# An adaLN block with linear attention and a mixture of experts on one core: scatters that wait for the one two tiles back, later last logits, full sixth down passes, a reordered first shared slot

## The reference, cut to what matters

```python
x: (4, 1024, 512) f32                       # B, N, C
mod = (silu(c) @ wmod) -> sa, ca, ga, sb, cb, gb     # ga, gb clamped away from 0
h = layernorm(x) * (1 + ca) + sa
x = x + ga * attention(h)                   # 16 heads of 32, relu(q), relu(k), linear:
                                            # (v_pad k^T) q, divided by its last row, then w_proj
h = layernorm(x) * (1 + cb) + sb
scores = sigmoid(h @ gate_w.T)              # 8 experts
idx = top_k(scores + router_bias, 2);  w = scores[idx] / sum(scores[idx])
out = sum_k w_k * (silu(h W1[e]) * (h W3[e])) W2[e]          # inner width 352
shared = (silu(h sw1.T) * (h sw3.T)) sw2.T                   # inner width 704
x = x + gb * (out + shared)
```

## Time and profile before

| | us |
|---|---|
| median of 3 runs | 1271.02 |
| lowest and highest | 1267.22, 1271.38 |
| profiled execution, its own time | 1265.33 |
| its span, first to last instruction | 1263.6 |
| TensorE busy in the span | 1202.6 (95%) |
| VectorE, ScalarE, GpSimd busy | 796.3, 416.6, 480.4 |

### The profile page before, as it was taken

How to read it: one execution, slowest core, us unless ns; L and a number is a source line. 1 busy time by engine, 2 the same in 40 slices (tenths; PEclk the granted TensorE clock), 3 DMA queues, 4 the chain that set the end, 5 groups by cost and what they waited for, 6 DMA issues and landing times.

```text
span 1263.6 us, 25262 instructions
## 1 busy us (share of the span) xinstructions
PE 1202.6 (95%) x9054; PEld 774.5 (61%) x9054; DVE 796.3 (63%) x1575; ACT 416.6 (33%) x873; POOL 480.4 (38%) x408
## 2 busy tenths in 40 slices
PE   7999999999998999999999999999999999999992
PEld 2646666666665666676776767566666555555551
DVE  6557778778765777476675643466666555555552
ACT  4324445444443333333332332222222222222220
POOL 2214566566554454311111102344443444344432
PEclk9999999999999999999999999999999999999996
DMA  7915698898788887453353443766766667777673
GB/s 232 234 44 150 169 220 207 214 231 202 190 209 188 221 201 177 105 131 94 93 141 84 103 128 77 164 126 126 126 126 126 125 126 121 131 126 122 118 108 46
DMA packets 253110, 185.01 MB, mean 146 GB/s; under 512 B 186480, under 2 KB 198768, under 8 KB 252988
## 3 DMA queue, kind: packets, MB, share of 16 engines
q1 hardware_dynamic: 217224, 114.14, 39.1%
q0 software_dynamic: 20512, 45.62, 20.9%
q10 hardware_dynamic: 15256, 23.62, 6.4%
HBM read 87.07 MB, written 52.49 MB: 110 GB/s over the span
## 4 chain that ended last, share of the span: by engine, by line
PE 37%; DMA 28%; issue 13%; POOL 11%; DVE 7%; ACT 2%; SPq 1%; POOLq 0%; ACTq 0%; DVEq 0%
DMA out<-y,slot_row 25%; PE ps_vs L86 3%; PE ps_vs L88 3%; PE ps_vs L87 3%; PE ps_vh L86 2%; PE ps_vh L88 2%; PE ps_vh L87 2%; POOL h L339 2%; PE ps_kh L86 2%; PE ps_kh L87 2%; PE ps_kh L88 2%; POOL xg L347 2%; POOL ol L352 2%; PE ps_qh L88 2%; PE ps_qh L86 2%
## 5 line engine op out<-in xcount | busy, mean ns | idle before, releaser
L428 POOL DMA_INDIRECT out<-y,slot_row x71 | 113.6, 1600 | 248.7 <-DMA out<-y,slot_row 223.1
L86 PE MATMUL ps_o<-w_all,xt 128*128 x568 | 177.8, 313 | 12.6 <-issue 12.3
L87 PE MATMUL ps_o<-w_all,xt 128*128 x568 | 177.6, 313 | 0.0
L88 PE MATMUL ps_o<-w_all,xt 128*128 x568 | 177.5, 313 | 0.0
L854 DVE SCALAR_TENSOR_TENSOR gate_row<-gate_rows,batch_weight,gate_row 128x512 f32<-128x512 f32 x213 | 158.9, 746 | 2.5
L366 POOL DMA_INDIRECT out<-s_sum,row_no x32 | 53.7, 1678 | 220.0 <-DVE s_sum L606 214.6
L861 DVE TENSOR_TENSOR y<-ps_vs,gate_row 128x512 f32<-128x512 f32 x71 | 49.1, 692 | 136.4 <-DMA out<-y,slot_row 118.0
L1105 ACT ACTIVATE at<-ps_y 128x384 f16<-128x384 f32 x71 | 34.9, 491 | 199.2 <-PE ps_y L1323 199.2
L328 POOL TENSOR_TENSOR h<-cen,rows_f 128x512 f32<-128x512 f32 x32 | 40.6, 1267 | 129.8 <-ACT cen L880 112.6
L1111 ACT ACTIVATE gate_row<-gate_rows,batch_weight 128x512 f32<-128x512 f32 x71 | 51.2, 722 | 115.2 <-DVE y L861 103.1
L86 PE MATMUL ps_qh<-ht,wqkv 128*128 128x128 f16 x512 | 87.4, 219 | 1.4 <-DVE wqkv L574 1.4
(11 more groups left out here) (247 smaller groups left out, 3321.3 us busy)
## 6 DMA issues: line engine op xcount, KB each, us to landing
w_stage<-in_w_d ACTq DMA_DIRECT2D x64, 176.0 KB, 2.6
xb<-in_x SPq DMA_DIRECT2D x32, 256.0 KB, 3.2
xr<-in_x SPq DMA_DIRECT2D x32, 256.0 KB, 3.7
out<-x SPq DMA_DIRECT2D x32, 256.0 KB, 3.4
h_d<-hl SPq DMA_DIRECT2D x32, 256.0 KB, 2.5
h2t_d<-h2t SPq DMA_DIRECT2D x32, 256.0 KB, 3.4
s_ht<-h2t_d SPq DMA_DIRECT2D x32, 256.0 KB, 3.5
sstage<-in_sh_flat SPq DMA_DIRECT2D x32, 136.0 KB, 3.2
```

What stands on the lines that cost most here:

```text
L86: nc.tensor.matmul(out, lh, rh, start=first, stop=False, skip_group_check=True)
L87: nc.tensor.matmul(out, lh, rl, start=False, stop=False, skip_group_check=True)
L88: return nc.tensor.matmul(out, ll, rh, start=False, stop=last, skip_group_check=True)
L428: pool.indirect_dma_start(m.out, bass.IndirectOffsetOnAxis(ap=m.slot_row[:, t:t + 1], axis=0), m.y[:, t % Y_RING, :], None, compute_op=ALU ...
```

## The change

Five edits.

1. Scatters. `scatter` of a tile waits for the scatter two tiles back. It waits for the last one too where the expert changes from tile t - 1 to tile t, and for the first tiles. There are two semaphores in turn. The number to wait for comes from a table `wait_for`, which `name_tiles` works out from the expert numbers and GpSimd reads into a register; a step of the semaphore `clear_of_last` follows. Padding slots of even and odd tiles name two different sets of 128 spare rows, so `out` has 128 rows more, and SyncE fills both sets.
2. TensorE's register load of the expert number is made once a tile, ahead of `e_turn`, and kept for `e_down`.
3. The last tile's logits move from the end of slot 43 to behind `up(TAIL_STEPS + 1)`. ScalarE's `logits_out` and the sigmoid, and VectorE's routing parts follow later: sum of logits at step TAIL_STEPS + 2, bias and first pick at + 4, second pick at + 5, weights at + 6, ranks at + 8 (RANK_STEP), run sums at + 14, masks from + 17; the listing ends 6 steps later.
4. The second sixth down pass takes all 128 rows, which adds low activations times low weights.
5. First shared slot (s = 32): GpSimd's `wp_scale` comes behind `o_low`, and ScalarE's `wp_high` moves to the slot's end.

```diff
-TURNS_FROM = TAIL_STEPS + 11
+RANK_STEP = TAIL_STEPS + 8
+TURNS_FROM = RANK_STEP + 9
...
     def scatter(t):
+        if 1 <= t < 3:
+            pool.wait_ge(m.scattered[(t - 1) % 2], 16)
+        if t >= 3:
+            pool.wait_ge(m.scattered[(t - 1) % 2], pool.value_load(m.wait_for[0:1, t:t + 1], min_val=16, max_val=ring_use(t - 1, 2)))
+            pool.sem_inc(m.clear_of_last, 1)
+            pool.wait_ge(m.clear_of_last, t - 2)
+        if t >= 2:
+            pool.wait_ge(m.scattered[t % 2], ring_use(t - 2, 2))
         pool.wait_ge(m.ey_ready, t + 1)
-        at_least(pool, m.scattered, 16 * t)
...
-                                compute_op=ALU.add).then_inc(m.scattered, 16)
+                                compute_op=ALU.add).then_inc(m.scattered[t % 2], 16)
...
+        step(v.tensor_tensor(m.other[:, :], m.eidf[:, 1:SLOT_TILES], m.eidf[:, 0:SLOT_TILES - 1], ALU.not_equal))
+        step(v.scalar_tensor_tensor(out=m.other[:, :], in0=m.other[:, :], scalar=16.0, in1=m.landed_two_back[:, 1:SLOT_TILES],
+                                    op0=ALU.mult, op1=ALU.add))
+        step(v.tensor_copy(m.wait_for[:, 1:SLOT_TILES], m.other[:, :]))
...
-    beside = {TAIL_STEPS: (bias_scores,), TAIL_STEPS + 2: (pick_first,), TAIL_STEPS + 3: (pick_second,), TAIL_STEPS + 4: (weigh,),
-              TAIL_STEPS + 8: (add_runs,), TAIL_STEPS + 9: (place,), TAIL_STEPS + 10: (name_slots,), LIST_STEP: (list_tokens,),
-              LIST_STEP - 1: (name_tiles,)}
-    sum_logits()
+    beside = {TAIL_STEPS + 2: (sum_logits,), TAIL_STEPS + 4: (bias_scores, pick_first), TAIL_STEPS + 5: (pick_second,),
+              TAIL_STEPS + 6: (weigh,), RANK_STEP + 6: (add_runs,), RANK_STEP + 7: (place,), RANK_STEP + 8: (name_slots,),
+              LIST_STEP: (list_tokens,), LIST_STEP - 1: (name_tiles,)}
...
     def e_out(t):
-        at_least(v, m.scattered, 16 * (t - Y_RING + 1))
+        if t >= Y_RING:
+            v.wait_ge(m.scattered[(t - Y_RING) % 2], ring_use(t - Y_RING, 2))
...
-        for b, k in wp_turn(s):
-            wp_high(b, k)
+        if s < TILES:
+            for b, k in wp_turn(s):
+                wp_high(b, k)
...
             convert_weights(q + 1)
-    logits_out(TILES - 1)
+            for b, k in wp_turn(s):
+                wp_high(b, k)
...
     for q in range(TAIL_STEPS, EARLY_STEPS):
         activate(q)
         high(q - 1)
+        if q == TAIL_STEPS + 2:
+            logits_out(TILES - 1)
+        if q == TAIL_STEPS + 3:
+            score()
...
-            nc.tensor.matmul(out, m.s_at[0:SH_HALF, j, 0, tok], m.sh[0:SH_HALF, 1, lo:lo + C], start=False, stop=True, ...)
+            nc.tensor.matmul(out, m.s_at[:, j, 0, tok], m.sh[:, 1, lo:lo + C], start=False, stop=True, ...)
...
         up(q)
-        if q == TAIL_STEPS + 6:
+        if q == TAIL_STEPS + 1:
+            logits(TILES - 1)
+        if q == RANK_STEP:
...
-    e_up(0)
+    expert = expert_of(0)
+    e_up(0, expert)
     down(CHUNKS - 1)
     for t in range(1, SLOT_TILES):
+        following = expert_of(t)
         e_turn(t - 1)
-        e_up(t)
+        e_up(t, following)
-        e_down(t - 1)
+        e_down(t - 1, expert)
+        expert = following
```

More of the change, by code:

```diff
@@ L224, in shared_step @@
             sp.wait_ge(m.s_gb_loaded, 48)
-            sp.dma_start(m.out[T:T + P, :], m.s_gb[:, 0, :]).then_inc(m.spare_stored, 16)
+            for j in range(2):
+                sp.dma_start(m.out[T + j * P:T + (j + 1) * P, :], m.s_gb[:, 0, :]).then_inc(m.spare_stored, 16)
         if j == 4 and n in (BT // 2 + 1, BT + 1):
@@ L448, in gpsimd_program @@
         gather(t + G_RING + 1)
-    pool.wait_ge(m.scattered, 16 * SLOT_TILES)
+    for j in range(2):
+        pool.wait_ge(m.scattered[j], ring_uses(SLOT_TILES, j, 2))
 def vector_program(nc, m, v):
@@ L808, in list_tokens @@
         step(v.tensor_scalar(m.weightf[:, :], m.weightf[:, :], 0.0, None, ALU.is_le))
-        step(v.tensor_scalar(m.rowf[:, :], m.tokenf[:, :], -1.0, m.spare_row[:, 0:1], ALU.mult, ALU.add))
+        step(v.scalar_tensor_tensor(out=m.rowf[:, :], in0=m.tokenf[:, :], scalar=-1.0, in1=m.spare_row[:, 0:SLOT_TILES], op0=ALU.mult, op1=ALU.add))
         step(v.tensor_tensor(m.rowf[:, :], m.rowf[:, :], m.weightf[:, :], ALU.mult))
@@ L1076, in scalar_program, with score @@
             convert_weights(q + 1)
-    logits_out(TILES - 1)
-    for j in range(X2_RING):
-        act.wait_ge(m.x2_stored[j], ring_uses(TILES, j, X2_RING))
-    for j in range(2):
-        act.wait_ge(m.hl2_stored[j], ring_uses(TILES, j, 2))
-    for j in range(H2T_RING):
-        act.wait_ge(m.h2t_stored[j], ring_uses(TILES, j, H2T_RING))
-    act.wait_ge(m.logits_ready, 1)
-    act.activation(m.scores[:, :, :], m.logits[:, :, 0:E], ACT.Sigmoid).then_inc(m.scores_ready, 1)
+            for b, k in wp_turn(s):
+                wp_high(b, k)
+    def score():
+        for j in range(X2_RING):
+            act.wait_ge(m.x2_stored[j], ring_uses(TILES, j, X2_RING))
+        for j in range(2):
+            act.wait_ge(m.hl2_stored[j], ring_uses(TILES, j, 2))
+        for j in range(H2T_RING):
+            act.wait_ge(m.h2t_stored[j], ring_uses(TILES, j, H2T_RING))
+        act.wait_ge(m.logits_ready, 1)
+        act.activation(m.scores[:, :, :], m.logits[:, :, 0:E], ACT.Sigmoid).then_inc(m.scores_ready, 1)
     for q in range(TAIL_STEPS, EARLY_STEPS):
@@ L1244, in down @@
             nc.tensor.matmul(out, m.s_at[:, j, 0, tok], m.sh[:, 0, lo:lo + C], start=False, stop=False, skip_group_check=True)
-            nc.tensor.matmul(out, m.s_at[0:SH_HALF, j, 0, tok], m.sh[0:SH_HALF, 1, lo:lo + C], start=False, stop=True, skip_group_check=True).then_inc(m.sy_done, 1)
+            nc.tensor.matmul(out, m.s_at[:, j, 0, tok], m.sh[:, 1, lo:lo + C], start=False, stop=True, skip_group_check=True).then_inc(m.sy_done, 1)
     pe.wait_ge(m.rep_done, KC)
@@ L1284, in tensor_program @@
             project_out(t - 1)
-        logits(t - 3)
+        if t - 3 < TILES - 1:
+            logits(t - 3)
     for q in range(TAIL_STEPS, EARLY_STEPS):
         up(q)
-        if q == TAIL_STEPS + 6:
+        if q == TAIL_STEPS + 1:
+            logits(TILES - 1)
+        if q == RANK_STEP:
             pe.wait_ge(m.both_ready, 1)
@@ L1305, in expert_of, with e_up @@
         return pe.value_load(m.eid[0:1, t:t + 1], min_val=0, max_val=E - 1)
-    def e_up(t):
-        expert = expert_of(t)
+    def e_up(t, expert):
         pe.wait_ge(m.xt_loaded[t % G_RING], ring_use(t, G_RING))
@@ L1324, in e_turn, with e_down @@
         mm.then_inc(m.at_done, 1)
-    def e_down(t):
-        expert = expert_of(t)
+    def e_down(t, expert):
         pe.wait_ge(m.e_at_lo, t + 1)
@@ L1485, in place_buffers @@
     m.eidf = sb("eidf", [1, SLOT_TILES], F32)
+    m.other = sb("other", [1, SLOT_TILES - 1], F32)
+    m.landed_two_back = sb("landed_two_back", [1, SLOT_TILES + 1], F32)
     m.lane_no = sb("lane_no", [P, P], F16)
@@ L1640 @@
     handles = {k: nc.dram_tensor(f"in_{k}", v.shape, mybir.dt.from_np(v.dtype), kind="ExternalInput").ap() for k, v in arrays.items()}
-    out = nc.dram_tensor("out_0", (T + P, C), F32, kind="ExternalOutput").ap()
+    out = nc.dram_tensor("out_0", (T + 2 * P, C), F32, kind="ExternalOutput").ap()
     adaln_block(nc, out=out, **handles)
```

25 lines of the change are left out of this document (16 added, 9 removed).

## The result

| | before | after |
|---|---|---|
| median, us | 1269.12 (4 runs, 1264.63 to 1271.38) | **1217.82** (4 runs, 1217.66 to 1218.70) |
| profiled execution, its own time | 1265.33 | 1217.89 |
| its span | 1263.6 | 1216.1 |
| TensorE busy | 1202.6 (95%) | 1189.8 (98%) |

The change takes 0.9601 of the time before, 95% interval 0.9571 to 0.9632. The forecast was 1221.0, the range 1212 to 1237. The total came out as forecast; one of the reasons behind it did not, as the experiments show.

A forecast was written before the change was run, and what follows sets the result against it. TensorE bounds the kernel first, then GpSimd's chain of scatters, each awaiting the last one's landing. Gains 34.5 + 3.1 + 2.8 + 1.2 + 6.6 = 48.2 from 1265.33 give 1217.1; plus 3.8, forecast 1221 us, range 1212 to 1237.

The forecast's parts named there:

- Scatters two back, 34.5: Expert stage: two scatters in flight let TensorE keep 5.855 us a tile, so the end comes 34.5 us earlier.
- TensorE's own loads, nothing: Expert stage: TensorE's register loads of the expert number show only where it was waiting, so no separate gain.
- Do two scatters slow each other?: Expert stage: two scatters in flight land no later than one alone, as the shared stage's pairs do; priced at nothing.
- First shared slot, 3.1: First shared slot: ScalarE's activation no longer waits for GpSimd's wp_raw; 3.1 us gained, between 0 and 5.3.
- Last logits 2.8: Last tile's logits: other projections come first and cover TensorE's wait for the transposed tile; 2.8 us gained.
- router 1.2: Router's later steps: VectorE's work there holds TensorE up less; 1.2 of 1.63 us gained, between 1.6 gained and 2 lost.
- Sixth passes, 6.6: Ends of shared down projections: with 128 rows in all sixth passes, 0.41 us goes 16 times; 6.6 us gained.
- The rival that rests on the Trainium skill's rule on weight loads: Sixth down passes: rows don't matter, the slow place has another cause and the 6.6 stays; 1227.5 us, chance 0.13.
- The offset of 3.8: Whole kernel: 3.8 us added to the profiled-execution sum, the middle of the median's 5.7 and the fastest run's 1.9.
- The pace stays: Expert stage rival: two scatters in flight take as long as two in turn, only 13.7 gained; 1257 us, chance 0.04.
- GpSimd as the bound: Expert stage rival: register load, wait and semaphore step make GpSimd's loop slower than before; 1333 us, chance 0.02.
- DMA engines: Expert stage rival: transfers delay one another, the pace settles at 6.08 us a tile; 1237 us, chance 0.10.

## Why the prediction was right, and where it was not

**The bound.** "TensorE then keeps 5.855 us to the end": 5.853. The last scatter came 47.1 us earlier (1255.64 to 1208.53) where the sum said 48.2. The kernel is bound by TensorE to the end now.

**Scatters two back, 34.5, and TensorE's own loads, nothing: these two steps were wrong and made up for one another.** The sentence that failed is that the loads "cost nothing while TensorE is the bound and show only where it was waiting". I took their price from tiles in which the scatters drift past TensorE's turns, and then made a change that holds them in one place. With the loads where they were, the scatters give 23.6 in the kernel before, and the whole change without the early loads stands at 1227.2; moving the loads is worth 9.4. The forecast came out because it priced the loads' exposure at nothing and the diff contains the edit that makes it nothing. That is luck and not foresight. Together the two edits shorten the way from the first to the last scatter by 32.7 us (440.05 to 407.39), close to the 34.5.

**Do two scatters slow each other?** For the scatters themselves "nothing" held: they do not fall behind and y never waits for one. There is little to test here, since they start 5.85 us apart (median) and land after some 5.5. What I had not on my list was TensorE's load, which takes longer in a stretch behind each scatter. GpSimd's own load was priced at nothing, and that held too: in the run where it stands between y and the scatter, the scatter starts 2.05 instead of 1.48 us after y's start, all of it in idle time.

**First shared slot, 3.1:** undone, 3.2, and this agreement is partly luck. The slot's second hole stayed, as said (2.51 for 2.64). But the holes of the run that undid the edit give only 2.2 more than those of the changed kernel; the other part is the fall of TensorE's clock behind them, which the sum has not. I had looked at the granted clock only in the three stretches of the earlier trace rows, and in the profile of before it was 0.57 over the 4 us behind this slot's second hole.

**Last logits 2.8, router 1.2:** undone, 4.9 for 4.0. The hole went. Of the router's 1.63 some 0.2 were gained instead of 1.2, because 0.76 came up at a second down projection (before had a second one too, of 0.40). The largest term left, 1.66, was not in the sum: TensorE's clock mostly falls behind that hole, and the profile of before was an execution in which it did not.

**Sixth passes, 6.6:** undone, 6.7. The rival that rests on the Trainium skill's rule on weight loads (TensorE: Matmul & The Clock Gate, "LDWEIGHTS (loading the stationary operand)") falls. What the Trainium skill says of a change of tiling mode, that it drains the engine (TensorEngine Tiling (Array Packing), "Key Properties"), fits the step at 64 rows; that such a pass is a change of mode no row shows. "Long at every change of rows and nowhere else" was too wide: passes of 96 rows behind 128 cost nothing more, in the run with 96 rows and in the down passes of the kernel before's own expert stage.

**The offset of 3.8 was mis-sized:** the sum on the profiled execution was 1217.1, the profiled execution of after took 1217.89, and the median is 0.07 below that. It came from the median of three executions, 1271.02, and that median was high: beside the experiments the kernel before had medians of 1263.1 to 1265.6 in 7 to 16 executions, so there was hardly an offset from the profiled 1265.33 to add. The chain of scatters need not explain it. Four runs of after lie within 1.0 us, and those of each run that keeps the two-back waits and the early loads within 4.1; with the chain back they spread over 6.9, and the kernel before over 13 in sixteen executions.

**Two of the rivals' times stand on another base.** "The pace stays" at 1257 and GpSimd as the bound at 1333 were counted down or up from the median of 1271, the forecast from 1265.33 + 3.8. On the forecast's base they are some 2 us less; nothing hangs on it.

**DMA engines:** I expected a share of 0.75 at the new pace and saw 0.80 to 0.85, with a few bytes more per us (130 to 137 GB/s for 123 to 127). TensorE was not held up by them, so the rival fell, though the engines are nearer to full than I had thought. Its price, a pace of 6.08, is close to the 6.01 of the exposed loads, which is why a total alone could not have told these two apart.

**Scatter starts after y:** 1.48 us behind y's start, where the sum had it at y's end, 0.69 behind; with the last tile's down passes starting 1.75 after its transposes instead of 1.92, it is 5.4 from the last transposes to the last scatter instead of 4.8 us.

## What to carry to other kernels

A short load of a register in front of an engine's own stream is hidden only as long as its latency stays below its cover. Its latency is not constant: in this kernel it is longer at one distance behind a scatter, so a change that fixes that distance can expose it in every other tile. Measure it under the timing that the change will bring, or move it out of the way together with the change, one load per tile ahead of the wait that stands there anyway. Two edits of one diff can hold each other's price, so undo each by itself even where the total came out as forecast. Two things that one run changes together are not yet told apart: before you name what two transfers do to each other, check that both are in flight at that moment, and look for the same delay where only one is. A hole is worth more than its length where the clock falls behind it, so read the granted clock behind each hole and not only over long stretches. And where the two-back wait removed the chain of landings, the spread from run to run shrank with it, while more buffers without it changed nothing.

## What the runs showed of the hardware

- A register load of TensorE took about 0.9 us at the start of the expert stage and up to 2.1 in it (1.22 of cover and 0.91 to the up pass with the two-back wait; 0.60 and 1.39 in tile 41 of the kernel before, where scatters go one at a time).
- With a cover of 1.2 us it came late only where the scatter's instruction on GpSimd ended 1.9 to 2.9 us ahead of the transposes: 111 of 208 tiles there, none of 125 elsewhere, over seven profiles.
- Matmul passes of 64 rows behind passes of 128 rows, and the reverse, start 0.31 to 0.32 us later instead of 0.22; behind and ahead of passes of 96 rows it is 0.22.
- Behind a hole of 2.8 us on TensorE the granted clock was 0.58 over the next 3.97 us, and the fall cost 1.66 us. Four of five profiles have it behind that hole; behind a single hole of 2.5 us in the first shared slot it is two of eight.
- GpSimd's accumulating scatter takes 2.03 us (median) in the changed kernel and 1.57 in the one before and in the run where a register load stands between the wait for y and the scatter. What sets this stayed open; it lay in idle time.
